# Residual LSTM and RNN on one core: bias copy and x sums reissued, the second layer's turn taken from PSUM

## What is computed

```python
# layer 0, an LSTM (Wx, Wh are 512 x 2048), c0 = 0
a = x_t @ Wx + b + prev_h @ Wh
i, f, o = sigmoid(a[:, :512]), sigmoid(a[:, 512:1024]), sigmoid(a[:, 1024:1536]); g = tanh(a[:, 1536:])
next_c = f * prev_c + i * g;  next_h = o * tanh(next_c)
x = x + hs                      # y0
# layer 1, a plain RNN (Wx, Wh are 512 x 512)
h_next = tanh(h @ Wh + x_t @ Wx + b)
x = x + hs                      # y1, the result
```

## Time and profile before

| | us |
|---|---|
| median of 3 runs | 2277.07 |
| lowest and highest | 2273.94 and 2279.57 |
| the profiled execution | 2289.59 |
| its span | 2287.8 |

### The profile page before, as it was taken

How to read it: one execution, slowest core, us unless ns; L and a number is a source line. 1 busy time by engine, 2 the same in 40 slices (tenths; PEclk the granted TensorE clock), 3 DMA queues, 4 the chain that set the end, 5 groups by cost and what they waited for, 6 DMA issues and landing times.

```text
span 2287.8 us, 148190 instructions
## 1 busy us (share of the span) xinstructions
PE 2210.8 (97%) x63548; PEld 1835.4 (80%) x63548; DVE 2100.8 (92%) x11050; ACT 1782.7 (78%) x6431; POOL 116.1 (5%) x143
## 2 busy tenths in 40 slices
PE   3899999999999999999999999999999999999996
PEld 1688888888888888888888888888888888888885
DVE  6899999999999999999998999899999999899997
ACT  3688787887887788777887788778887888778885
POOL 4000000000000000000000000000000000000000
PEclk7999999999999999999999999999999999999998
DMA  5000000000000000000000000000000000000000
GB/s 209 3 23 23 18 23 14 18 22 23 18 23 13 18 23 22 18 16 19 18 23 21 19 13 23 18 23 18 23 13 18 23 23 18 22 14 18 23 13 12
DMA packets 16733, 53.88 MB, mean 24 GB/s; under 512 B 2256, under 2 KB 2384, under 8 KB 14800
## 3 DMA queue, kind: packets, MB, share of 16 engines
q1 hardware_dynamic: 16080, 44.41, 5.4%
HBM read 27.62 MB, written 16.78 MB: 19 GB/s over the span
## 4 chain that ended last, share of the span: by engine, by line
PE 95%; DVE 2%; issue 1%; ACT 1%; DMA 1%; POOL 0%; SPq 0%; DVEq 0%; ACTq 0%; POOLq 0%
PE in_ps L244 24%; PE rnn_ps L244 22%; PE rec_first_ps L244 20%; PE rec_second_ps L244 19%; PE c_ps L244 10%; DVE wh_part L452 1%; DMA x_sb<-xT 1%; ACT wh_part L658 0%; DVE turned L483 0%; DVE wh_parts L452 0%; POOL x_sums L211 0%; ACT wh_parts L658 0%; DVE largest_slice L407 0%; ACT gates_cell L693 0%; DVE pre_sb L489 0%
## 5 line engine op out<-in xcount | busy, mean ns | idle before, releaser
L244 PE MATMUL rec_first_ps<-wh_part,h_parts 128*32 128x256 f16 x16352 | 561.2, 273 | 20.7 <-DVE h_parts L536 20.6
L244 PE MATMUL rec_second_ps<-wh_part,h_parts 128*32 128x256 f16 x16352 | 560.9, 273 | 0.1
L244 PEld LDWEIGHTS rec_first_ps<-wh_part,h_parts 128*32 128x32 f16 x16352 | 436.3, 96 | 59.5 <-issue 32.2
L244 PEld LDWEIGHTS rec_second_ps<-wh_part,h_parts 128*32 128x32 f16 x16352 | 469.0, 97 | 1.1 <-issue 0.3
L244 PE MATMUL in_ps<-wx_sums,x_sums 128*32 128x256 f32 x6096 | 417.3, 379 | 2.2 <-issue 1.2
L244 PEld LDWEIGHTS rnn_ps<-wx_sb,y 128*32 128x32 f32 x8192 | 249.7, 109 | 156.4 <-issue 126.8
L693 ACT ACTIVATE gates_cell<-gate_ps,unscale 128x128 f32<-128x128 f32 x511 | 187.9, 368 | 240.3 <-DVE gate_ps L489 237.9
L244 PE MATMUL rnn_ps<-wx_sb,y 128*32 128x128 f32 x8192 | 347.6, 275 | 13.0 <-issue 6.3
L244 PE MATMUL rnn_ps<-wh_parts,h_parts 128*32 128x256 f16 x8176 | 344.8, 274 | 8.2 <-DVE h_parts L571 8.2
L244 PEld LDWEIGHTS in_ps<-wx_sums,x_sums 128*32 128x32 f32 x6096 | 225.2, 110 | 92.7 <-issue 4.7
L244 PEld LDWEIGHTS rnn_ps<-wh_parts,h_parts 128*32 128x32 f16 x8176 | 249.9, 97 | 11.4 <-issue 8.5
(11 more groups left out here) (93 smaller groups left out, 3575.8 us busy)
## 6 DMA issues: line engine op xcount, KB each, us to landing
x_sb<-xT SPq DMA_DIRECT2D x32, 512.0 KB, 4.1
yT<-y SPq DMA_DIRECT2D x64, 256.0 KB, 2.4
wh_sb<-wh SPq DMA_DIRECT2D x5, 1024.0 KB, 9.0
wx_sb<-wx SPq DMA_DIRECT2D x5, 1024.0 KB, 14.4
b_sb<-b SPq DMA_DIRECT2D x1, 256.0 KB, 2.7
b_sb<-b SPq DMA_DIRECT2D x1, 64.0 KB, 11.6
h_first<-h0T SPq DMA_DIRECT2D x1, 32.0 KB, 11.3
```

What stands on the lines that cost most here:

```text
L244: last = nc.tensor.matmul(out[QUAD * q:QUAD * (q + 1)], states, weights(q), start=False, stop=True, tile_position=(0, QUAD * q), skip_grou ...
```

## The change

It has four parts.

- **Bias copy.** `bias1` is issued right behind `seed1` on ScalarE, ahead of `gates(0)`, instead of behind `tanh_cell(0)`.
- **Sums of x.** `sum_x` runs in steps 3, 4, 7 and 8 of a chunk instead of 3, 4, 5 and 6, and waits for the low state of the step before (`h0_ready[1]`) instead of the first half's matmuls of the same step (`rec0_done[0]`).
- **Layer 1's sums.** ScalarE's `copy_low1` and VectorE's `sum1` go. `turn1` turns all 256 columns of `rec1_ps` straight from PSUM into `turned1`, `halve1` adds blocks 0, 1 to blocks 2, 3 (128 columns out, both inputs in SBUF), and `add1` adds the two halves of that (64 columns). `seed1` now waits for `turned1_done` where it waited for `rec1_summed`.
- **VectorE's order.** In parts 0 and 1 (called early): turn1, halve1, turn0(0), add1, add0(0), turn0(1). In parts 2 and 3 (late): turn1, begin_c12 or finish_c22, turn0(0), halve1, add0(0), add1, turn0(1).

```diff
+STEPS_OF_X_SUMS = (3, 4, 7, 8)
...
-                if 3 <= c < 7 and v + 1 < CHUNKS:
-                    pool.wait_ge(rec0_done[0], t + 1)
-                    sum_x(v + 1, c - 3)
+                if c in STEPS_OF_X_SUMS and v + 1 < CHUNKS:
+                    pool.wait_ge(h0_ready[1], t)
+                    sum_x(v + 1, STEPS_OF_X_SUMS.index(c))
...
-            def sum1(s):
-
-                dve.wait_ge(rec1_copied, s + 1)
-                nc.vector.tensor_tensor(rec1_sum[:, :, :], rec1_by_part[:, :, 0], rec1_low[:, :, :],
-                                        ALU.add).then_inc(rec1_summed, 1)
-
             def turn1(s):
 
-                dve.wait_ge(rec1_summed, s + 1)
-                nc.vector.transpose(turned1[:, :].rearrange("p b n -> p (b n)"),
-                                    rec1_sum[:, :].rearrange("p b c -> p (b c)")).then_inc(turned1_done, 1)
+                dve.wait_ge(rec1_done, s + 1)
+                nc.vector.transpose(turned1[:, :].rearrange("p b r n -> p (b r n)"), rec1_ps).then_inc(turned1_done, 1)
+
+            def halve1(s):
+
+                dve.wait_ge(turned1_done, s + 1)
+                nc.vector.tensor_tensor(half1[:, :, :], turned1[:, :, 0:2], turned1[:, :, 2:4], ALU.add).then_inc(half1_done, 1)
 
             def add1(s):
-                dve.wait_ge(turned1_done, s + 1)
-                nc.vector.tensor_tensor(slices(pre1[:, :]), turned1[:, :, 0:BATCH], turned1[:, :, BATCH:],
-                                        ALU.add).then_inc(pre1_done, 1)
+                dve.wait_ge(half1_done, s + 1)
+                nc.vector.tensor_tensor(slices(pre1[:, :]), half1[:, :, 0], half1[:, :, 1], ALU.add).then_inc(pre1_done, 1)
...
+                sums_early = not lstm or t >= SLOTS or part < 2
                 if rnn:
-                    sum1(s)
+                    turn1(s)
+                    if sums_early:
+                        halve1(s)
                 if lstm and t < SLOTS:
                     if part == 2:
                         begin_c12(g, t)
                     elif part == 3:
                         finish_c22(g, t)
-                if rnn:
-                    turn1(s)
                 if lstm:
                     turn0(0, t)
                 if rnn:
+                    if sums_early:
+                        add1(s)
+                    else:
+                        halve1(s)
+                if lstm:
+                    add0(0, n)
+                if rnn and not sums_early:
                     add1(s)
                 if lstm:
-                    add0(0, n)
                     turn0(1, t)
...
                 if s:
-                    act.wait_ge(rec1_summed, s)
+                    act.wait_ge(turned1_done, s)
...
-            def copy_low1(s):
-                act.wait_ge(rec1_done, s + 1)
-                nc.scalar.activation(rec1_low[:, :, :], rec1_by_part[:, :, 1], ACT.Copy).then_inc(rec1_copied, 1)
...
-                if s >= 1:
-                    copy_low1(s - 1)
...
                 if 0 <= s < STEPS:
                     seed1(s)
+                if s >= 0 and s % 2 and s // 2 + 2 < PAIRS:
+
+                    act.wait_ge(seed1_done, s + 1)
+                    bias1(s // 2 + 2)
                 if t < STEPS:
                     gates(0, t)
...
                     tanh_cell(0, t)
-                if s >= 0 and s % 2 and s // 2 + 2 < PAIRS:
-
-                    act.wait_ge(seed1_done, s + 1)
-                    bias1(s // 2 + 2)
```

More of the change, by code:

```diff
@@ L89, in residual_lstm_rnn @@
         pre0_sb, tanh_c_sb = sb("pre0_sb", [P, BLOCKSH * BATCH]), sb("tanh_c_sb", [P, CELLH])
-        rec1_low, rec1_sum = sb("rec1_low", [P, SUB, QUAD]), sb("rec1_sum", [P, SUB, QUAD])
-        turned1 = sb("turned1", [P, SUB, 2 * BATCH])
+        turned1, half1 = sb("turned1", [P, SUB, 4, BATCH]), sb("half1", [P, SUB, 2, BATCH])
         pre1 = sb("pre1", [P, CELL])
@@ L135, in residual_lstm_rnn @@
         rec1_done, turned1_done, pre1_done = sem("rec1_done"), sem("turned1_done"), sem("pre1_done")
-        rec1_copied, rec1_summed = sem("rec1_copied"), sem("rec1_summed")
+        half1_done = sem("half1_done")
         h1_full_done, h1_high, h1_ready, y1_done = (
```

## The result

The changed kernel takes 2212.5 us (median of 4 runs, 2212.2 to 2213.11) against 2278.32 for the kernel before, measured beside it: a ratio of 0.9715, 95% interval 0.9698 to 0.9731. That is 65.8 us faster. The forecast was 2234, 44 us faster, with a range down to 2218: right in sign, too high in time, and outside its range. Its profiled execution took 2213.11 us (span 2211.3), close to its median, while the profiled execution of the kernel before, 2289.59, lay 11 us above its own.

A forecast was written before the change was run, and what follows sets the result against it. With the bias stall gone, the recurrence was taken to bound the kernel: 1.48 us a chunk gave 47 us, less about 4 for scattered delays, so 2246.6 us profiled, scaled to 2234; range 2218 to 2259.

The forecast's parts named there:

- What bounds the kernel: Whole step: the recurrence sets a floor of 4.15 us a step; TensorE's own, taken as 4.13, lies just below.
- Bias copy: ScalarE, odd steps: TensorE's stall of 0.19 us goes and the step falls to 4.15, gaining 1.20 us a chunk.
- Sums of x: GpSimd against VectorE: sums stop holding layer 1's addition, and holding halve1 stays hidden, gaining 0.39 us a chunk.
- Layer 1's sums, late steps: VectorE, parts 2 and 3: the second turn comes 0.03 us later on the recurrence, losing 0.24 us a chunk.
- Scattered delays: Delays without named cause, 31 us in all, stay; those the bias wait swallowed now count, taking about 4 us off.
- A: VectorE becomes the bound in late steps, halve1 and add1 delaying the second turn: 2299 us at the upper bound; chance 0.08.
- B: VectorE's collision with GpSimd's sum is not hidden, so 4 x 0.10 us a chunk is not gained: 2246; chance 0.12.
- C: TensorE's changeovers set another floor, steps staying at 4.17 us early and 4.21 late: 2247; chance 0.12.
- D: ScalarE's bias move does nothing, odd steps stay at 4.30 us and only the sums count: 2273; chance 0.06.
- The scale: Whole kernel: the profiled execution stands 0.55% above the median of 2277.07, so the profiled forecast of 2246.6 became 2234.

## Why the prediction missed, step by step

**What bounds the kernel: right.** The recurrence's floor of 4.15 stands in all four parts (4.148), so TensorE's own is not above it. Where the second turn came later, by 0.13 us with the early order everywhere, the step grew by 0.12.

**Bias copy: mechanism and size right for the undisturbed steps.** The step put 1.20 us a chunk on it, and 0.02 on each of the 8 even steps, 0.16. The bias copy alone shortened the chunk by 1.41.

**Sums of x: right.** 0.39 forecast, 0.42 alone and 0.37 on top of the bias copy (66.71 to 66.34). The halving was held as foreseen and stayed off the path; the sum began at +0.43, within the bounds given. The lock that the Trainium skill's page describes ("SBUF — State Buffer", "SBUF: two separate sides") agrees: in the changed kernel the halving ends 0.14 us after the sum, in the one with layer 1's sums alone 0.15, and layer 1's addition in the kernel before 0.08. What such a meeting costs the step was 0, 0.30 and 0.10 us, by the slack behind it.

**Layer 1's sums, late steps: mis-sized.** I took 0.03 us a late step, 0.24 a chunk, 7.6 us in all. Measured: 0.00. The second turn starts at +1.99, and at +1.98 in the early step, whose additions lie ahead of it. I had charged 0.21 from the halving to the next addition, the trace shows 0.17, and I had no row for the halving, so I added three rounded distances with no slack. With the bias copy moved the whole part is worth nothing (2211.21 without it, 2212.5 with it). With the bias copy where it was, it takes away some 10 us of scattered delays, which the prediction did not see.

**Scattered delays: the step that failed.** The prediction said that they would stay and that 4 us more of them would show, because "scattered delays in odd steps were partly swallowed by the bias wait". The opposite happened: about 10 us of them went in the medians and 20 in the traces. In the medians 10 + 4 + 8.9 = 22.9 us of better account stand against the 22.8 by which the gain of 65.8 exceeds the 43 forecast. In the traces, these 20, the 4 not paid and 8.9 from the undisturbed chunk (66.64 against 66.36) account for the 33.5 us between the 2246.6 forecast for a profiled execution and the 2213.11 measured (20.2 + 4 + 8.9 = 33.1). I had read 31 us of delay as a constant of the kernel because the trace names no cause for it (5 of them are the first 17 steps), and treated a stop as a buffer.

What the runs showed in its place: the delays last only where TensorE's stop for the bias and ScalarE's copy, with its wait for layer 1's matmuls in front of the seeds, are both there. Taking away either one is enough. A disturbed step of the kernel before, 1220.78 to 1225.46 (4.68 us), shows what they look like. The first row belongs to the step before: TensorE stops in the midst of `units`, for no semaphore that the profile shows. Then its column tiles are out of step, layer 1's matmuls end 0.6 us into the next step, and the copy, the sum and the turn wait for them, one after another.

```profile
1219.20 0.41 PE L244 MATMUL in_ps<-wx_sums,x_sums 128*32 128x256 f32 x2 [0.32 <-issue]
...
1221.05 0.31 PE L244 MATMUL rnn_ps<-wh_parts,h_parts 128*32 128x256 f16 x2
...
1221.39 0.28 ACT L684 ACTIVATE rec_low<-rnn_ps 128x128 f32<-128x128 f32 x1 [0.64 <-PE rnn_ps L244]
...
1221.70 0.29 DVE L550 TENSOR_TENSOR rec_sum<-rnn_ps,rec_low 128x128 f32<-128x128 f32 x1 [0.91 <-ACT rec_low L684]
...
1222.46 0.41 DVE L483 STREAM_TRANSPOSE turned<-rec_first_ps 128x256 f32<-128x256 f32 x1
```

The first turn starts at +1.68 here, at +1.33 in the undisturbed step of rows 4, which has a 256-column addition of VectorE too. In the kernel before such stretches last ten steps and more; in the changed one a disturbance dies out within a few.

The copy put back reached VectorE by no dependence and brought the delays back all the same, so the way through VectorE is not needed and ScalarE's queue alone will do. What TensorE's `units` wait for stands there behind the copy. The seed itself is done in time: in steps of part 2, where `units` wait for nothing of ScalarE's behind it, it ends 0.46 us or more before TensorE's first weight load of `units`. The close one is `begin_c11` in part 1: with the copy put back it ends 0.07 us before that load (median), without the copy 0.61. In the kernel with the bias copy alone moved it is 0.11, and the delays are gone, so being close is not enough. That the delays travel this way was not tested, and whether it is the wait or the 0.31 us of the copy itself was not separated.

A long stretch is also not one hiccup handed on. TensorE stops anew in it: in the kernel before, for example, in steps 154, 156, 158, 160, 162 and 164. Counted over steps 18 to 499, in one execution of each kernel, two matmul starts in `units` or in front of an even step's `input1` lie more than 0.24 us apart in 35 steps of the kernel before, in 24 with the copy put back, in 15 with the sums of x alone, and in 0 to 6 of every other kernel, 0 of the changed one. The waits on "issue" of the weight loads of `units` show the difference (us in total, times, longest), first before, then after; the one of 15 us is of the start:

```profile
PEld c_ps L244 <- issue: 21.9, 17, 15.1
PEld in_ps L244 <- issue: 13.3, 31, 0.9
```

```profile
PEld c_ps L244 <- issue: 16.0, 5, 15.0
PEld in_ps L244 <- issue: 2.3, 7, 1.0
```

These stops go with the loading of instructions. The page lists a DMA queue that carries nothing else, here as number of packets, MB and share; the trace has one packet of it about every 4.3 us, 0.9 to 1.7 us long where such a stop follows:

```profile
q8 instruction: 503, 8.24, 1.5%
```

In all of the 35, 24 and 15 steps TensorE went on 1.2 to 1.7 us after the end of such a packet, while of all matmul starts of `units` and `input1` in the kernel before only some 12% lie so. So the likely reading is that TensorE had run out of instructions. No run changed how they are loaded, so this is not shown. Why the stop for the bias and the copy, together, bring it about stays open.

**The rivals.** A (VectorE the bound) needs 0.215 us a late step; it was 0.00, and 0.12 with the early order everywhere. B (a collision not hidden) costs 11 to 23 us when the sum is put where it used to be, and nothing where the change put it. C and D did not happen: undisturbed steps take 4.148 and the odd ones are no longer than the even. The range failed because its low end, 2218, allowed the undisturbed steps their best but held the scattered delays fixed.

**The scale.** I carried a difference of a profiled execution over to the median by a ratio. By the account above the excess of 11 us of that execution was itself scattered delay (20 went in the traces, 10 in the medians), which the change removes; the changed kernel's profiled execution lies at its median.

## What to carry to other kernels

- Count the undisturbed step and what lies above it apart, and don't take the second as a constant: ask whether these delays are still there when a stop of the bottleneck or an in-order wait of another engine has gone. Here taking away either one of two was enough, and the traces alone would not have said so.
- When a stall goes, price the next limit from the same step (here 0.15 of the 0.19 could be had), and a collision by the slack of what it delays, not by its own length.
- Run each part of a change by itself: here two changes of order gave all of the 66 us, and the rewritten sums nothing on top of them.

## What the hardware did that was not expected

- VectorE starts an independent addition 0.17 us after the halving of 128 columns (1101.37 to 1101.54) and 0.20 after another addition of that size (1101.54 to 1101.74); that halving lasts 0.25 us there, and 0.29 in the median of all 512 steps.
- An addition with two SBUF inputs that meets a sum on GpSimd ends 0.14 to 0.15 us after it with 128 columns and 0.08 with 64 (1114.75 + 0.48 against 1114.42 + 0.73).
- TensorE's column tiles can run out of step: matmuls of layer 1 still start at 1221.05, 0.27 us after the next step's first matmul at 1220.78, and ScalarE's copy waits for the last of them.
- TensorE's stops without a semaphore in `units` end 1.2 to 1.7 us after a packet of the instruction queue, in each of the 74 steps of three kernels that have one over 0.24 us.
